# A filter's base moved to GpSimd and its steps reordered on ScalarE and VectorE

## The reference

```python
# first block, on n = _gn(x)
a = n @ Wa + ba
b = n @ Wb + bb
g = sigmoid(n @ Wg + bg)
ab = einsum('bijk,bikl->bijl', a, b)     # per image and channel a 64x64x64 product
x1 = x + (g * ab) @ Wo + bo
# second block: a 4x4 filter on the image dilated by two, stride two, per channel
x2 = x1 + depthwise_conv(_gn(x1), filt, lhs_dilation=2, window_strides=2)
```

## Time and profile before

| what | us |
|---|---|
| median of 3 runs | 71.86 (71.24 to 71.92) |
| the profiled execution, its own time | 70.91 |
| span of its trace | 69.1 |

### The profile page before, as it was taken

The page is one execution under the profiler, slowest core; times in us unless marked ns, Lnnn a source line. Parts: engine busy times, 40 slices in busy tenths (PEclk is TensorE's granted clock), DMA queues, the critical chain, the costliest instruction groups (busy, mean ns, idle before and its releaser), DMA issues.

```text
span 69.1 us, 1800 instructions
## 1 busy us (share of the span) xinstructions
PE 52.8 (76%) x708; PEld 40.1 (58%) x708; DVE 43.4 (63%) x123; ACT 32.3 (47%) x55; POOL 38.4 (56%) x49
## 2 busy tenths in 40 slices
PE   4999898769899975979977898787398947786000
PEld 4988785539569845847853866574286832362000
DVE  0183699793537895337599533769944299993650
ACT  5200033254730043399369465938906499261500
POOL 1000376399996099996930496292069419659500
PEclk9999999999999999999999999999999999999955
DMA  0999960000000000000012004002100400030084
GB/s 0 308 264 342 372 250 0 0 9 0 0 0 0 9 0 5 0 0 9 0 47 104 0 0 152 9 0 82 70 9 5 152 0 0 33 119 5 0 303 152
DMA packets 2600, 4.86 MB, mean 70 GB/s; under 512 B 288, under 2 KB 416, under 8 KB 2592
## 3 DMA queue, kind: packets, MB, share of 16 engines
q1 hardware_dynamic: 2592, 4.75, 19.8%
HBM read 2.66 MB, written 2.10 MB: 69 GB/s over the span
## 4 chain that ended last, share of the span: by engine, by line
PE 27%; POOL 19%; DVE 17%; issue 12%; ACT 10%; POOLq 0%; DVEq 0%; ACTq 0%
PE ps_o L640 8%; POOL y L243 7%; PE ps_b L598 7%; POOL rstd L214 6%; ACT y L316 5%; POOL gn L230 4%; PE ps_t L566 4%; DVE x L431 4%; PE ps_ag L608 4%; ACT gate L303 2%; PE ps_ag L587 2%; DVE part L376 2%; DVE y L447 2%; ACT prod L325 2%; DVE y L441 2%
## 5 line engine op out<-in xcount | busy, mean ns | idle before, releaser
L243 POOL TENSOR_TENSOR y<-y,prod 128x512 f32<-128x512 f32 x12 | 15.3, 1272 | 13.0 <-DVE y L441 10.3
L214 POOL TENSOR_TENSOR rstd<-veps,half 128x2 f32<-128x2 f32 (+1 forms) x7 | 5.7, 810 | 10.6 <-DVE veps L406 10.6
L237 POOL TENSOR_TENSOR xb<-xs,par 128x512 f32<-128x512 f32 x8 | 10.1, 1286 | 1.6 <-issue 1.6
L303 ACT ACTIVATE gate<-ps_ag,par 128x512 f32<-128x512 f32 x8 | 5.5, 687 | 10.6 <-PE ps_ag L608 10.5
L290 ACT ACTIVATE rt<-ps_t 128x512 f32<-128x512 f32 x7 | 4.2, 596 | 11.9 <-PE ps_t L566 11.9
L598 PE MATMUL ps_b<-par,rt 128*128 128x128 f32 x64 | 8.8, 281 | 0.0
L413 DVE TENSOR_TENSOR bsb<-ps_b,par 128x512 f32<-128x512 f32 x8 | 5.5, 689 | 4.7 <-PE ps_b L598 4.7
L539 PE MATMUL ps_ag<-zeros 128*128 128x128 f32 x46 | 7.6, 327 | 1.0 <-DVE zeros L450 1.0
L640 PE MATMUL ps_o<-par,zt 128*64 128x128 f32 x112 | 7.7, 278 | 0.6 <-DVE x L431 0.6
L598 PEld LDWEIGHTS ps_b<-par,rt 128*128 128x128 f32 x64 | 7.8, 192 | 0.3 <-issue 0.3
L422 DVE TENSOR_TENSOR zt<-ps_ab,gate 128x512 f32<-128x512 f32 x8 | 5.4, 677 | 3.9 <-ACT gate L303 3.0
(11 more groups left out here) (57 smaller groups left out, 76.3 us busy)
## 6 DMA issues: line engine op xcount, KB each, us to landing
xs<-x SPq DMA_DIRECT2D x8, 256.0 KB, 5.0
out<-y SPq DMA_DIRECT2D x8, 256.0 KB, 2.0
par<-params SPq DMA_DIRECT2D x1, 417.5 KB, 4.5
par<-params SPq DMA_DIRECT2D x1, 128.0 KB, 3.1
```

What stands on the lines that cost most here:

```text
L214: nc.gpsimd.tensor_tensor(job_of(rstd, job), job_of(veps, job), half[:, 0:columns(job)], ALU.pow).then_inc(rstd_done, 1)
L237: nc.gpsimd.tensor_tensor(xb[:, w, b, :, :], xs[:, w, b, :, :], bo.broadcast_to([128, ROWS, D]), ALU.add).then_inc(xb_ready, 1)
L243: return nc.gpsimd.tensor_tensor(y[:, w, b, :, :], y[:, w, b, :, :], prod[:, n % 2, k, :, :], ALU.add)
L303: nc.scalar.activation(gate[:, g % 2, :, :], ps_ag[:, :, 256:512], ACT.Sigmoid, bias=bcol[:, 1:2]).then_inc(gate_ready, 1)
```

## The change

GpSimd makes the base of image 0 of waves 0 to 2, in a new `filter_base(w)` right behind `filter_coefs(w)`. ScalarE still makes that of image 1 (`filter_base1`). Two semaphores, `base0_ready` and `base1_ready`, replace `base_ready`.

On ScalarE the four products of a wave and base 1 stand elsewhere: in unit 2w+4 after `a_out` come the two products of image 0, then the gate, then base 1; in unit 2w+5 after `a_out` comes the first product of image 1, then the transposes' copies and the gate, then the second product of image 1, then `halo_out`. For wave 2 all five stand after the last unit. On VectorE `filter_right(w, 0)` moves from the end of unit 2w+3 to unit 2w+4, behind `b_out` and ahead of `x1_out(w+1, 1)`; for wave 2 it moves from ahead of `x1_out(3, 0)` to behind `aggregate` of the last wave, and `filter_right(2, 1)` moves from ahead of `deviation` to behind it. No DMA is moved in the list of SyncE.

```diff
+            def filter_base(w):
+                pool.wait_ge(coef_ready, w + 1)
+                nc.gpsimd.tensor_scalar(y[:, w, 0, :, :], x1[:, w, 0, 0:ROWS, 0:D], coef[:, w, 0, 0:1], beta[:, w, 0:1],
+                                        ALU.mult, ALU.add).then_inc(base0_ready, 1)
...
             filter_coefs(0)
+            filter_base(0)
             add_bo(3)
             add_products(0, 0)
             add_products(0, 1)
             filter_coefs(1)
+            filter_base(1)
             add_products(1, 0)
             add_products(1, 1)
             filter_coefs(2)
+            filter_base(2)
             add_products(2, 0)
...
-            def filter_products(w, b):
+            def filter_product(w, b, k):
                 n = 2 * w + b
+                act.wait_ge(coef_ready, w + 1)
+                act.wait_ge(halo_ready, w + 1)
                 if n >= 2:
                     act.wait_ge(add_done, n - 1)
-                act.wait_ge(halo_ready, w + 1)
-                for k in range(2):
-                    nc.scalar.activation(prod[:, n % 2, k, :, :], x1[:, w, b, 1:ROWS + 1, k:D + k], ACT.Copy,
-                                         scale=coef[:, w, b, k + 2:k + 3]).then_inc(prod_ready, 1)
+                nc.scalar.activation(prod[:, n % 2, k, :, :], x1[:, w, b, 1:ROWS + 1, k:D + k], ACT.Copy,
+                                     scale=coef[:, w, b, k + 2:k + 3]).then_inc(prod_ready, 1)
...
                 a_out(g)
-                if n == 1 and w + 1 < WAVES:
-                    transposed_out(w + 1, 0)
-                    transposed_out(w + 1, 1)
-                gate_out(g)
-                if n == 1 and w >= 1:
-                    halo_out(w - 1)
-                if g >= 3:
-                    filter_base((g - 3) // 2, (g - 3) % 2)
-                if g == UNITS - 1:
-                    filter_base(LAST - 1, 1)
-                if g >= 3:
-                    filter_products((g - 3) // 2, (g - 3) % 2)
-            filter_products(LAST - 1, 1)
+                if n == 0:
+                    if w >= 2:
+                        filter_product(w - 2, 0, 0)
+                        filter_product(w - 2, 0, 1)
+                    gate_out(g)
+                    if w >= 2:
+                        filter_base1(w - 2)
+                else:
+                    if w >= 2:
+                        filter_product(w - 2, 1, 0)
+                    if w + 1 < WAVES:
+                        transposed_out(w + 1, 0)
+                        transposed_out(w + 1, 1)
+                    gate_out(g)
+                    if w >= 2:
+                        filter_product(w - 2, 1, 1)
+                    if w >= 1:
+                        halo_out(w - 1)
+            filter_product(LAST - 1, 0, 0)
+            filter_product(LAST - 1, 0, 1)
+            filter_base1(LAST - 1)
+            filter_product(LAST - 1, 1, 0)
+            filter_product(LAST - 1, 1, 1)
...
                     b_out(g)
+                    if w >= 2:
+                        filter_right(w - 2, 0)
                     x1_out(w - 1, 1)
...
-                    if g >= 5:
-                        filter_right((g - 5) // 2, 1)
+                    if w >= 2:
+                        filter_right(w - 2, 1)
                     variance(X1JOB + w - 1)
                     b_out(g)
                     z_out(g)
-                    filter_right((g - 3) // 2, 0)
             job = X1JOB + LAST
             x1_out(LAST, 0)
             x1_out(LAST, 1)
             x1_part(LAST)
             aggregate(job)
+            filter_right(LAST - 1, 0)
+            deviation(job)
             filter_right(LAST - 1, 1)
-            deviation(job)
```

More of the change, by code:

```diff
@@ L133, in preact_pair_mix_blur @@
         pad_ready, halo_done, halo_ready = sem("pad_ready"), sem("halo_done"), sem("halo_ready")
-        coef_ready, base_ready, prod_ready = sem("coef_ready"), sem("base_ready"), sem("prod_ready")
+        coef_ready, prod_ready = sem("coef_ready"), sem("prod_ready")
+        base0_ready, base1_ready = sem("base0_ready"), sem("base1_ready")
         right_ready = sem("right_ready")
@@ L312, in halo_out, with filter_base1 @@
                 last.then_inc(halo_ready, 1)
-            def filter_base(w, b):
+            def filter_base1(w):
                 act.wait_ge(coef_ready, w + 1)
-                nc.scalar.activation(y[:, w, b, :, :], x1[:, w, b, 0:ROWS, 0:D], ACT.Identity,
-                                     bias=beta[:, w, b:b + 1], scale=coef[:, w, b, 0:1]).then_inc(base_ready, 1)
-            def filter_products(w, b):
+                nc.scalar.activation(y[:, w, 1, :, :], x1[:, w, 1, 0:ROWS, 0:D], ACT.Identity, bias=beta[:, w, 1:2],
+                                     scale=coef[:, w, 1, 0:1]).then_inc(base1_ready, 1)
+            def filter_product(w, b, k):
                 n = 2 * w + b
+                act.wait_ge(coef_ready, w + 1)
+                act.wait_ge(halo_ready, w + 1)
                 if n >= 2:
                     act.wait_ge(add_done, n - 1)
-                act.wait_ge(halo_ready, w + 1)
-                for k in range(2):
-                    nc.scalar.activation(prod[:, n % 2, k, :, :], x1[:, w, b, 1:ROWS + 1, k:D + k], ACT.Copy,
-                                         scale=coef[:, w, b, k + 2:k + 3]).then_inc(prod_ready, 1)
+                nc.scalar.activation(prod[:, n % 2, k, :, :], x1[:, w, b, 1:ROWS + 1, k:D + k], ACT.Copy,
+                                     scale=coef[:, w, b, k + 2:k + 3]).then_inc(prod_ready, 1)
             transposed_out(0, 0)
@@ L436, in filter_right @@
             def filter_right(w, b):
-                n = 2 * w + b
-                dve.wait_ge(base_ready, n + 1)
+                dve.wait_ge((base0_ready, base1_ready)[b], w + 1)
                 dve.wait_ge(pad_ready, w + 1)
@@ L501, in _ @@
                 else:
-                    deviation(X1JOB + w - 1)
-                    if g >= 5:
-                        filter_right((g - 5) // 2, 1)
+                    if w >= 1:
+                        deviation(X1JOB + w - 1)
+                    if w >= 2:
+                        filter_right(w - 2, 1)
                     variance(X1JOB + w - 1)
```

## The result

| | us |
|---|---|
| kernel before, median of 4 runs | 71.55 (71.10 to 71.92) |
| changed kernel, median of 4 runs | 74.88 (73.90 to 76.78) |
| ratio | 1.042, 95% interval 1.029 to 1.056 |
| changed kernel, profiled execution: own time, span | 75.0, 73.2 |

All ratios here leave out the executions that took over 1.5% longer than the fastest of their kernel. Forecast were 73.7 and a range of 72.5 to 74.7. The direction was right; the median lies 0.2 above the range. The mean granted clock of the four executions was 0.943, 0.970, 0.890 and 0.947, and the one at 0.970 took 73.90: the clock turns out to be part of the answer.

What follows compares the result with a forecast made beforehand. The prediction took the kernel to be bound by hand-overs, no engine being full. It summed -0.33 us to the end of X1 and +2.13 after it to +1.80 on the 71.86 median: 73.7, range 72.5 to 74.7.

Steps and rivals of the forecast that it cites:

- Base 0 on GpSimd: Image 0's base made by GpSimd: 0.77 us each, taken from a same-shape row; the first one costs nothing.
- Unit 4, +0.24: filter_right(0,0) between b_out(4) and x1_out(1,1) ends at 34.90; x1_out(1,1) starts at 34.82, 0.24 us later.
- Unit 5 and the neighbour row: Image 1's second product delays halo_out(1); product_o(2,0) starts at 43.0, not 42.40, eating the removed 0.60 us stall.
- Unit 6, +0.28: filter_right(1,0) waits for b_out(6) and base 0, both at 45.9; x1_out(2,1) starts at 46.60 instead of 46.32.
- Unit 7: All 0.28 us later, product_o(3,0) +0.35; x1_out(3,1), no longer behind a sum, starts at 56.35: -0.33 us.
- The end, 8.09 us behind X1: After X1, three GpSimd adds and three VectorE sums alternate; the last inverse root ends at 65.12 instead of 63.32, +1.80 us.
- The 0.55: VectorE's two-input sum ends about 0.55 us after the GpSimd instruction blocking it, as each waits for the other's whole instruction.
- the 1.12: In the end's turns, a blocked GpSimd add still streams 1.12 us: 1.27 less 0.15 already done.
- The second, no exclusion: Rival: VectorE and GpSimd do not exclude each other, only GpSimd's list counts: root +0.74, 72.6 us; chance 0.12.
- The third, the loop at TensorE's pace: Rival: stalls of 0.43, 0.60 and 0.92 us vanish without new delays, X1 ends at 54.7; 71.4 us; chance 0.07.
- The first: Rival: loop loses too, by a 1.27 us base or late coefficients holding unit 6's gate: 74.2 to 74.6; chance 0.16.
- the sum of +1.80: Whole change: -0.33 us to the end of X1 and +2.13 from there, making +1.80.

Runs made afterwards that it cites:

- two series: The changed kernel, unedited, measured in its first four executions and again in six more: ratio to the kernel before 1.042, then 1.053.
- with idle products: Changed kernel plus TensorE products of zeros into an unread bank, two ahead of unit 7's first statistics product, five behind: 73.29 to 73.56 us, ratio 1.027.
- that part alone: Kernel before with only the changed VectorE order of wave 2's filter_right sums: 76.88, 72.68, 75.33 and 75.56 us.
- the filled scratch tile: Changed kernel with idle TensorE products in unit 7, GpSimd's three adds ahead of the last inverse root replaced by fills reading nothing: ratio 0.999 to kernel before.

## Why the prediction was right or wrong

- **Base 0 on GpSimd, 0.77 us, at no cost.** Right: a row of 0.77 each, and a ratio of 0.997 alone.
- **Unit 4, +0.24.** Right. The sum (34.75 in the trace after) ended 0.08 into `x1_out(1,1)`, at 35.41, or 34.81 less the start; written was 34.82.
- **Unit 5 and the neighbour row.** Right, with TensorE's wait of 0.36 at 43.61 and the row at 43.01 less the start, where 43.0 was written. The second add of (0,1) ran at 43.20, or 42.6; written was 42.5. The early product, put back, removed both.
- **Unit 6, +0.28.** It was +0.35. Base and `b_out` met within 0.1 us, as worked out (the sum at 46.61, or 46.01; written was 45.93).
- **Unit 7.** The neighbour row's wait of 0.54 at 56.64 was there as well. But the sentence "all is 0.28 later" took TensorE's speed as given. That step failed: in 9 of 10 executions of the changed kernel the mean clock was under 0.96, and in both traces B's product in unit 7 took 1.92 us. The prediction put the clock at nothing without a reason beyond the trace before, where it was full in all slices but the last two, though by its own working TensorE's gaps grew (from 0.23 to 0.64 ahead of the statistics product, as measured). It is the term that puts the median above the range: 74.9 and 75.7 in two series, against 73.4 with idle products. Where the clock stays up, X1 ended at 57.15 for my 57.03.
- **The end, 8.09 us behind X1.** Measured 8.06, and 8.05 with that part alone. The turns came in the order written: three adds with sums between them in 4.62 us (61.66 to 66.28), the sums 1.24, 1.75 and 1.56 long, the root 1.04. The 0.55 that was read off four rows of the kernel before, and the 1.12 worked out from them, carried it: counted from the end of X1, the ends of the three sums and of the root came within 0.05 us of the places written.
- **The rivals.** The second, no exclusion, fell by the filled scratch tile; its price, 7.03, is what that run comes to by the estimate with its fills as long as adds. The third, the loop at TensorE's pace, didn't come: the stalls of 0.43 and 0.92 were there unchanged. The first did not come either: the base took 0.77, and the thin cover in unit 6 held, with ScalarE idle for 0.41 us ahead of the gate at 47.48.

So the sum of +1.80 stands against +1.8 to +1.9 (73.4 to 71.63 or 71.5) for the work itself, and the clock adds 1.5 to 2.3 to it.

## What to carry to other kernels

When an operation moves down one engine's list, ask first who starts only once it is done: here a sum that is in nobody's way on VectorE held back two adds of GpSimd that had lain beside the statistics, and they came to stand ahead of the last inverse root. Work that another engine can do only while VectorE reads one operand from SBUF has to be placed there; moved behind the root it cost the same time again. And a kernel with gaps on TensorE can lose as much by the granted clock (here 1.5 to 2.3 us) as by the change itself, so that a forecast wants a term for it, and the experiments a version of both kernels with the gaps filled.

## What the runs showed of the hardware

- VectorE's operations with two operands in SBUF and GpSimd's additions take turns, one whole instruction each, also when both have several in a row (1.24, 1.75, 1.56 us beside adds, against 0.75 alone). Beside a GpSimd fill that reads nothing they take 0.74 to 0.75. Both agree with the Trainium skill (SBUF — State Buffer, Who interferes with whom), which limits the conflict to a GpSimd instruction that reads SBUF.
- A GpSimd inverse root of 128x2 that came while such a sum ran ended 0.56 us behind it, but it added only 0.11 us to two sums that stood around it.
- A GpSimd fill of 128x1024 fp32 took 0.95 us, an addition of 128x512 1.27, a scale-and-add of 128x512 0.77.
- TensorE's granted clock fell from 1.0 (2.4 GHz) to 0.5 (1.2 GHz) in or behind stretches in which TensorE had waited, for 3.4 us in eight cases of the kept traces and for 6.8 in one. The product for B took 1.92 us there instead of 1.06, and one fall in unit 7 cost 1.6 us. How often it falls differs between kernels with the same gaps there, and the runs don't show why.
